# Attention scores of two layers from two extra projection columns, carried as bf16 pieces, in a four-layer graph network on one core

## What is computed

```
L0: h @ W;  e = leaky_relu(h@a[:D] + (h@a[D:])^T);  att = softmax(where(adj > 0, e, NEG), axis=1)
    elu(att @ (h @ W)) @ han_w + han_b
L1: e_r[i,j] = sum_d h[i,d] h[j,d] a_rel[r,d] + c_r;  the relation is chosen by adj; softmax; att @ h
L2: Wh = h @ W^T;  e = leaky_relu(Wh@a1 + (Wh@a2)^T);  softmax(where(adj == 0, NEG, e));  att @ Wh
L3: three steps of  m = h @ weight[i];  aggr = (adj != 0)^T @ m;  h = gru_cell(aggr, h)
```

## Time and profile before

| | us |
|---|---|
| median of 3 runs | 563.78 |
| lowest, highest | 562.48, 564.67 |
| the profiled execution's own time | 562.25 |
| its span (what the views show) | 560.5 |
| mean granted clock of TensorE | 0.97 |

### The profile page before, as it was taken

One profiled execution on the slowest core, in us unless ns is written; L12 is line 12 of the kernel. 1 busy time (PEld: TensorE's weight loads), 2 busy tenths in 40 slices (PEclk: granted clock), 3 DMA queues, 4 the chain that ended last, 5 costly groups with the idle time before them and its releaser, 6 DMA issues.

```text
span 560.5 us, 10803 instructions
## 1 busy us (share of the span) xinstructions
PE 515.1 (92%) x3262; PEld 439.1 (78%) x3280; DVE 429.4 (77%) x1436; ACT 408.8 (73%) x956; POOL 363.5 (65%) x314
## 2 busy tenths in 40 slices
PE   5857876899999999999999999999999999999964
PEld 5856665788888888888888888888888777868753
DVE  3636786788888898888888888888888887867633
ACT  1563565778887878788888888797888677767742
POOL 4241764777787878868687877777877666463330
PEclk9896998999999999999999999999999999999987
DMA  7980000000000000000000000000000000000001
GB/s 188 253 236 1 2 1 1 1 2 2 1 2 19 0 19 0 19 0 19 0 19 0 19 0 19 0 11 8 0 19 0 19 2 20 20 1 20 0 20 37
DMA packets 20893, 14.00 MB, mean 25 GB/s; under 512 B 2944, under 2 KB 18048, under 8 KB 20864
## 3 DMA queue, kind: packets, MB, share of 16 engines
q1 hardware_dynamic: 18944, 13.25, 8.5%
q10 hardware_dynamic: 1920, 0.40, 0.4%
HBM read 9.44 MB, written 4.19 MB: 24 GB/s over the span
## 4 chain that ended last, share of the span: by engine, by line
PE 67%; ACT 13%; DVE 8%; issue 5%; DMA 4%; POOL 2%; ACTq 1%; POOLq 0%; DVEq 0%; another core or an unknown queue 0%
PE ps_mix L1174 7%; PE ps_L L1053 7%; PE ps_L L1151 5%; ACT prob_L L485 4%; PE ps_r L1180 3%; PE ps_r L1182 3%; PE ps_z L1182 3%; PE ps_z L1180 3%; PE ps_r L1181 3%; PE ps_z L1181 3%; PE ps_mix L1053 3%; DVE xn_L L720 3%; PE ps_L L1131 3%; DMA above_row<-above 2%; PE ps_L L1159 2%
## 5 line engine op out<-in xcount | busy, mean ns | idle before, releaser
L720 DVE SCALAR_TENSOR_TENSOR xn_L<-x_sb,stats_L,rstd_L 128x128 f32<-128x128 f32 x256 | 86.6, 400 | 9.4 <-POOL rstd_L L359 6.9
L379 POOL TENSOR_TENSOR hT_lo<-hTf,hT_hi 128x512 fp32r<-128x512 f32 x32 | 44.8, 1399 | 66.4 <-ACT hT_hi L566 66.4
L374 POOL TENSOR_TENSOR diff<-hTf,gate_r 128x512 f32<-128x512 f32 x48 | 62.3, 1297 | 33.2 <-ACT gate_r L560 33.2
L485 ACT ACTIVATE prob_L<-prob_L,negm_L 128x128 f32<-128x128 f32 x192 | 74.3, 392 | 1.6 <-DVE negm_L L757 1.5
L359 POOL TENSOR_TENSOR rstd_L<-veps_L,minus_half 128x4 f32<-128x4 f32 x64 | 71.3, 1114 | 5.3
L403 POOL TENSOR_SCALAR mask_L<-adj_sb 128x512 bf16<-128x512 int32 (+1 forms) x32 | 65.9, 2058 | 2.7
L795 DVE TENSOR_TENSOR ag_lo<-ps_mix,ag_hi 128x512 fp32r<-128x512 f32 x48 | 33.2, 692 | 32.8 <-ACT ag_hi L533 32.8
L1174 PE MATMUL ps_mix<-adj_sb,hN 128*128 (+1 forms) x384 | 52.6, 281 | 1.0 <-ACT hN L572 0.8
L549 ACT ACTIVATE gate_r<-ps_r,bias_r 128x512 f32<-128x512 f32 x48 | 33.0, 687 | 27.1 <-PE ps_r L1182 25.6
L1174 PEld LDWEIGHTS ps_mix<-adj_sb,hN 128*128 128x128 f32 x384 | 49.6, 197 | 3.1 <-ACT hN L572 1.6
L757 DVE CUSTOM_DVE_ANT_0 prob_L<-ps_L,prob_L 128x128 f32<-128x128 f32 x192 | 44.0, 284 | 7.4 <-issue 7.3
(11 more groups left out here) (168 smaller groups left out, 1564.0 us busy)
## 6 DMA issues: line engine op xcount, KB each, us to landing
out_dram<-x_sb SPq DMA_DIRECT2D x16, 256.0 KB, 2.3
x_sb<-in_x_dram SPq DMA_DIRECT2D x1, 768.0 KB, 11.8
adj_sb<-in_adj_dram SPq DMA_DIRECT2D x1, 768.0 KB, 12.2
x_sb<-in_x_dram SPq DMA_DIRECT2D x2, 256.0 KB, 6.0
adj_sb<-in_adj_dram SPq DMA_DIRECT2D x2, 256.0 KB, 7.1
w_ih_sb<-in_L_gnn_w_ih_dram SPq DMA_DIRECT2D x1, 192.0 KB, 8.4
w_hh_sb<-in_L_gnn_w_hh_dram SPq DMA_DIRECT2D x1, 192.0 KB, 3.6
w_l_sb<-in_L_gnn_weight_dram SPq DMA_DIRECT2D x1, 192.0 KB, 3.2
```

What stands on the lines that cost most here:

```text
L374: nc.gpsimd.tensor_tensor(diff[k][:, :], hTf[k][:, :], gate_r[k][:, :], ALU.subtract).then_inc(diff_done[k], 1)
L379: nc.gpsimd.tensor_tensor(hT_lo[k + 1][:, :], hTf[k + 1][:, :], hT_hi[k + 1][:, :].bitcast(F32), ALU.subtract).then_inc(new_hT_lo[k], 1)
L485: last = nc.scalar.activation(part(prob[s], b), part(prob[s], b), ACT.Exp, bias=negm[s][:, b:b + 1], scale=-1.0, accum_out=psum_row[s][:, ...
L720: last = nc.vector.scalar_tensor_tensor(part(xn[s], b), graph(x_sb, g, b), stats[s][:, b, 1:2], rstd[s][:, b:b + 1].to_broadcast([P, D]), ...
```

## The change

The two score numbers per node now come from the projection. The weight of layers 0 and 2 gets two more columns (`w_aug`, 128x130: the weight, and the two score vectors times 0.2), so that one projection gives values and both numbers. ACT copies all of it to SBUF (`copy_projected`; before, only layer 2's values were copied). DVE splits the eight numbers per node and group (4 graphs x 2) into three bf16 pieces each (`split`: 4 operations that each wait for the one before). PE transposes the 24 columns with one bf16 matmul (`pieces_transposed`), ACT copies the 24x128 result (`copy_pieces`), and PE makes the outer sum with eight bf16 matmuls of 24 rows, against `chosen`, constant tiles of zeros and ones that pick a graph's pieces. The mask matmuls stay.

In layer 0, `normalise` becomes `centre`: one operation that subtracts the mean and does not wait for the inverse deviation. The deviation goes in later: into the score numbers (a fifth step ahead of the split) and into the inverse of the sum (a second operation in `inverse_sum`).

PSUM: a projection of 4 x 130 columns needs more than a bank, so it takes halves of two neighbouring ones. The banks of layer 0, `ps_in` and layer 2 lie side by side in `ps_row`; the projections of layers 0 and 2 both use `ps_in`'s, in turn with three candidate products per period.

The flag: PE sums the counts over the partitions with matmuls of one column (`count_above`), and no transfer is left. DVE compares the sum. The time terms of layer 1 are made right after `add_layer_0(0)`.

POOL: `edges_in_place` now subtracts layer 2's mask from ones and follows it; seven or so more steps at the start make the constant tiles. The waits that were on `wait_alone` are on the instructions themselves in `norm_stats` and `leaky`.

Order: all hardware loops are gone. Each engine's program is a written list of calls; groups 8 to 15 repeat one pattern, written once and unrolled when it is built, and the start and the end are lists of their own. The bank a step waits for is an argument of the call. Cut to its core:

```diff
-    MIX_USES = (("a2", 5), ("a1", 4), ("t2", 5), ("a3", 5), ("t3", 6), ("t1", 4))
...
+    DA = D + 2
+    HALF = 2 * DA
+    NP = 3
+    NR = GB * NP
...
-        ps = {"L0": bank("ps_L0"), "L1": bank("ps_L1"), "L2": bank("ps_L2")}
+        ps_row = ctx.enter_context(nc.psum_tensor("ps_row", [P, 3 * W], F32))
+        ps = {"L0": ps_row[:, 0:W], "L1": bank("ps_L1"), "L2": ps_row[:, 2 * W:3 * W]}
         ps_mix, ps_r, ps_z = bank("ps_mix"), bank("ps_r"), bank("ps_z")
-        ps_in, ps_hn = bank("ps_in"), bank("ps_hn")
+        ps_in, ps_hn = ps_row[:, W:2 * W], bank("ps_hn")
...
-            for a, b in FLAG_SUMS:
-                sp.wait_ge(s_above, b)
-                sp.dma_start(above_row[:, 0:(b - a) * P], above[:, a:b]).then_inc(s_above_row, 16)
...
-            with sp.Fori(0, NG) as g:
+            for g in range(NG):
                 store(g)
...
             def rsqrt(s, g):
                 pool.wait_ge(stats_done[s], g + 1)
+                if s == "L0":
+                    wait_from(pool, rinv_done["L0"], g)
                 nc.gpsimd.tensor_scalar(veps[s][:, :], stats[s][:, :, 2], 1.0 / D, EPS, ALU.mult,
-                                        ALU.add).then_inc(veps_done[s], 1)
-                pool.wait_ge(veps_done[s], g + 1)
+                                        ALU.add).then_inc(rstd_done[s], 1)
...
-                nc.gpsimd.tensor_scalar(group(adj_sb, g).bitcast(F32), group(adj_sb, g), 0, 0,
-                                        ALU.is_equal, ALU.is_equal).then_inc(edges_done, 1)
...
+                nc.gpsimd.tensor_tensor(group(adj_sb, g).bitcast(F32), all_ones[:, :],
+                                        mask["L2"][:, :], ALU.subtract).then_inc(edges_done, 1)
...
+            def copy_projected(s, g):
+                act.wait_ge(values_in_psum[s], g + 1)
+                if s == "L2":
+                    wait_from(act, mixed["L2"], g)
+                nc.scalar.activation(projected_sb[s].rearrange("p b c -> p (b c)")
+                                     .rearrange("p (h c) -> p h c", h=2), projected_half(s),
+                                     ACT.Copy).then_inc(values_copied[s], 1)
...
+            def copy_pieces(s, g):
+                act.wait_ge(pieces_in_psum[s], g + 1)
+                nc.scalar.activation(piecesT[s][:, :], ps[s][0:2 * NR, W - D:W], ACT.Copy)\
+                    .then_inc(piecesT_done[s], 1)
...
+            def centre(g):
+                dve.wait_ge(stats_done["L0"], g + 1)
+                wait_from(dve, xT_in_psum["L0"], g)
+                nc.vector.tensor_tensor(by_graph(xn["L0"][:, :]), by_graph(group(x_sb, g)),
+                                        stats["L0"][:, :, 1:2].to_broadcast([P, GB, D]),
+                                        ALU.subtract).then_inc(xn_done["L0"], 1)
...
+                if s == "L0":
+                    dve.wait_ge(rstd_done["L0"], 2 * (g + 1))
+                    nc.vector.reciprocal(inverse_0[:, :], psum_row["L0"][:, :])\
+                        .then_inc(inverse_0_done, 1)
+                    dve.wait_ge(inverse_0_done, g + 1)
+                    nc.vector.tensor_tensor(rinv["L0"][:, :], inverse_0[:, :], rstd["L0"][:, :],
+                                            ALU.mult).then_inc(rinv_done["L0"], 1)
...
+            def split(s, g, before, whole):
+                piece = [pieces[s][:, :, :, n] for n in range(NP)]
+                step = split_step[s]
+                nc.vector.tensor_scalar(piece[0], whole, 1.0, None, ALU.mult).then_inc(step, 1)
+                dve.wait_ge(step, before + 1)
+                nc.vector.tensor_tensor(parts_left[s][:, :, :], whole, piece[0], ALU.subtract)\
+                    .then_inc(step, 1)
+                dve.wait_ge(step, before + 2)
+                nc.vector.tensor_scalar(piece[1], parts_left[s][:, :, :], 1.0, None, ALU.mult)\
+                    .then_inc(step, 1)
+                dve.wait_ge(step, before + 3)
+                nc.vector.tensor_tensor(piece[2], parts_left[s][:, :, :], piece[1], ALU.subtract)\
+                    .then_inc(step, 1)
+            def score_pieces_0(g):
+                dve.wait_ge(values_copied["L0"], g + 1)
+                dve.wait_ge(rstd_done["L0"], 2 * (g + 1))
+                before = SPLIT_STEPS["L0"] * g + 1
+                nc.vector.tensor_tensor(score_parts[:, :, :], projected_sb["L0"][:, :, D:DA],
+                                        rstd["L0"][:, :].unsqueeze(2).to_broadcast([P, GB, 2]),
+                                        ALU.mult).then_inc(split_step["L0"], 1)
+                dve.wait_ge(split_step["L0"], before)
+                split("L0", g, before, score_parts[:, :, :].rearrange("p b t -> p t b"))
+            def score_pieces_2(g):
+                dve.wait_ge(values_copied["L2"], g + 1)
+                split("L2", g, SPLIT_STEPS["L2"] * g,
+                      projected_sb["L2"][:, :, D:DA].rearrange("p b t -> p t b"))
...
             def read_flag(n):
-                a, b = FLAG_SUMS[n]
-                dve.wait_ge(s_above_row, 16 * (n + 1))
-                after_prep(nc.vector.tensor_reduce(above_max[:, :], above_row[:, 0:(b - a) * P],
-                                                   AX.X, ALU.max))
-                after_prep(nc.vector.tensor_scalar(many[:, :], above_max[:, :], 0.5, None,
-                                                   ALU.is_gt))
+                dve.wait_ge(above_counted, n + 1)
+                after_prep(nc.vector.tensor_scalar(many[:, n:n + 1], ps_z[0:1, 3 * D:3 * D + 1], 0.5,
+                                                   None, ALU.is_gt))
...
+                for b in range(GB):
+                    last = nc.tensor.matmul(projected_half(s)[:, b // 2, (b % 2) * DA:(b % 2 + 1) * DA],
+                                            part(hT[s], b), w_aug[s][:, :], start=True, stop=True)
+                last.then_inc(values_in_psum[s], 1)
...
+            def pieces_transposed(s, g):
+                if s == "L0":
+                    keep_clock_up(8, g)
+                pe.wait_ge(split_step[s], SPLIT_STEPS[s] * (g + 1))
+                nc.tensor.matmul(ps[s][0:2 * NR, W - D:W],
+                                 pieces[s][:, :, :, :].rearrange("p t b q -> p (t b q)"),
+                                 unit_b[:, :], start=True, stop=True).then_inc(pieces_in_psum[s], 1)
+            def piece_scores(s, b, stop):
+                nc.tensor.matmul(part(ps[s], b), part(chosen[0], b), piecesT[s][:, :],
+                                 start=False, stop=False)
+                return nc.tensor.matmul(part(ps[s], b), piecesT[s][:, :], part(chosen[1], b),
+                                        start=False, stop=stop)
             def scores_0(g):
-                keep_clock_up(3, g)
-                pe.wait_ge(hT_done["L0"], g + 1)
+                pe.wait_ge(piecesT_done["L0"], g + 1)
+                pe.wait_ge(values_copied["L0"], g + 1)
                 pe.wait_ge(mask_done["L0"], g + 1)
-                if isinstance(g, int) and g == 0:
-                    pe.wait_ge(s_prep_dve, PREP_L0)
-                nc.tensor.matmul(ps["L0"][:, :], a_src_rep[:, :], hT["L0"][:, :], start=True,
-                                 stop=False)
+                if g == 0:
+                    pe.wait_ge(s_prep_pool, N_PREP_POOL)
                 for b in range(GB):
-                    nc.tensor.matmul(part(ps["L0"], b), part(hT["L0"], b), a_dst_rep[:, :],
-                                     start=False, stop=False)
-                for b in range(GB):
-                    last = nc.tensor.matmul(part(ps["L0"], b), part(mask["L0"], b), ident_b[:, :],
-                                            start=False, stop=(b == GB - 1))
+                    nc.tensor.matmul(part(ps["L0"], b), part(mask["L0"], b), ident_b[:, :],
+                                     start=True, stop=False)
+                    last = piece_scores("L0", b, True)
...
             def scores_2(g):
-                pe.wait_ge(values_done["L2"], g + 1)
+                pe.wait_ge(piecesT_done["L2"], g + 1)
+                pe.wait_ge(values_copied["L2"], g + 1)
                 pe.wait_ge(mask_done["L2"], g + 1)
-                nc.tensor.matmul(ps["L2"][:, :], w2a_dst_rep[:, :], hT["L2"][:, :], start=True,
+                nc.tensor.matmul(ps["L2"][:, :], ident_b[:, :], mask["L2"][:, :], start=True,
                                  stop=False)
                 for b in range(GB):
-                    nc.tensor.matmul(part(ps["L2"], b), part(hT["L2"], b), w2a_src_rep[:, :],
-                                     start=False, stop=False)
-                nc.tensor.matmul(ps["L2"][:, :], ident_b[:, :], mask["L2"][:, :], start=False,
-                                 stop=True).then_inc(scores_done["L2"], 1)
...
+                    last = piece_scores("L2", b, b == GB - 1)
+                last.then_inc(scores_done["L2"], 1)
...
+            def count_above(first, last):
+                pe.wait_ge(s_above, last)
```

(8 more changed lines are left out.)

1800 lines of the change are left out of this document (1374 added, 426 removed).

## The result

The changed kernel takes **570.23 us** (median of 4 runs, 568.90 to 571.65), the kernel before, beside it on the same chip, 563.67 (4 runs, 562.48 to 564.67). The ratio is 1.0118, 95% interval 1.0084 to 1.0151: slower by 1.2%, where 6.5% faster was forecast. The profiled execution took 569.54 us, its span is 567.8.

What follows compares the result with a forecast made beforehand. PE alone was taken to bound the middle; from 560.5 us of span, middle -20.9, head -9 and tail -7 gave 523.6, a median of 527 us. The range, 8 times in 10, was 510 to 542.

Steps and rivals of the forecast that it cites:

- rival 3: Split chains lie open on PE, up to 4.5 us per group against 2.43 saved: slower, 585 us; chance 0.03.
- DVE's sum: DVE per group: -1.35 normalise, +0.69 centre, +1.60 tiny operations; 26.45 us busy, 26.8 with waits, 98% of PE's 27.24.
- PE's term for the new blocks: PE score blocks per group: layer 0's 12 short matmuls 0.57 us, layer 2's 0.61, priced at the mask's 0.048 each.
- upper bound, 28.2: PE's period if the weight load is not hidden behind 18 short matmuls, 0.97 us more than 27.24.
- Head: Start of the run: flag stall about -3 us, higher clock about -3, better filled order -3; -9 (0 to -16).
- terms on the flag: Head: PE's 4.11 us stall at the flag goes but for the register load, about -3 us; clock afterwards, about -3.
- POOL's set-up steps: Head: new steps ahead of group 0's xb and deviation, covered by DVE's angle work; uncovered up to 2 us.
- Tail: End of the run: layer 2's scores of three groups -4 us, less idle -3; -7 (-2 to -12).
- Rival 1: DVE takes over as bound at 0.2 us per tiny operation: 28.9 us period, total 540; chance 0.2.
- Rival 4: Unrolled code stalls at each skipped relation block, +30 us over 16 skips, result 557; chance 0.03.
- rival 2: The order gives back more: PE period 27.24, head -14, tail -10, total 514; chance 0.13.

Runs made afterwards that it cites:

- e1: Changed kernel with POOL's two-input GRU steps (diff, hT_lo) on 128 of 512 columns from group 1 on, leaving out work; 549.99 us, 0.9737 of before.
- e5: Changed kernel with layer 0's mask matmuls ahead of its pieces, plus calls reordered on four engines in the loop and the lists behind it; 565.2 us.
- e10: e8 with calls reordered in the loops of four engines, the lists behind nearly as they were; 545.23 us, 0.9645 of before.
- e6: Changed kernel with group 0's inverse deviation made between POOL's constant tiles and ACT's sine behind elu of group 0; 571.13 us.
- e8: Changed kernel with pieces padded by zeros so every score matmul has 128 rows, timed again after a single run; 558.80 us, 0.9903 of before.
- e2: Changed kernel with POOL's diff and hT_lo steps reading one tensor instead of two, subtraction left out; 555.09 us, 0.9837 of before.
- e4: Changed kernel with only the first bf16 piece made, six of nine split operations left out; 554.89 us, 0.9828 of before.

## Why the prediction was wrong

The forecast was 527 (510 to 542), with 0.94 on faster; the result lies 43 us above it. Of the cases named, only rival 3 was slower than before, and its mechanism was not the one. By the marks the forecast was -14.9 us over seven periods of 27.6 and -22 outside them; it came out as +3.4 and +4.0.

1. **The step that failed: DVE's sum, "so 26.45 busy … 26.8. That is 98% of PE's 27.24".** It moved DVE's operations into a new order and kept the durations they had beside their old neighbours. The operations themselves were, if anything, priced too high: without the held time DVE needs 29.25 - 4.65 = 24.6 us per period, against 26.45 less the 1.1 that before had. The tiny ones were nearly right (0.17 us and 0.02 to 0.04 between them). What came in place of the sum is 4.6 us per period of standing still behind POOL, 3.5 more than before. e1 takes 1.47 us off the period (30.21 to 28.74) with no change to DVE; e5 and e10 remove most of the hold by order alone.
2. **PE's term for the new blocks was mis-sized**: 1.49 for 0.57 in layer 0 and 0.86 for 0.61 in layer 2. "I take the lower, since the masks run at 0.048 with just such loads" took a row of 128-row matmuls for a case that changes rows eight times. PE's need per period is e1's 28.74 us, in which it idles 0.14; the sum had 27.24, and its upper bound, 28.2, was too low. The blocks are 1.17 of the 1.5 missing; the rest was not measured piece by piece. So of the 2.6 us per period by which the forecast missed, 1.14 are PE's (27.6 to e1's 28.74) and 1.47 the hold: 18 us over seven periods.
3. **Head, forecast -9, measured +7.8 by the first mark.** Its terms on the flag came true in kind and were outweighed. PE's longest idle time near the flag is 1.97 us for 4.11, and from 40 to 60 us the granted clock is 0.90 for 0.74:

```profile
41.59 0.38 PE L1859 MATMUL ps_L<-mask_L,ident_b 128*128 128x512 bf16 x1 [1.97 <-ACT arhT L623]
```

Two terms of the head failed. POOL's set-up steps were taken as covered by DVE's angle work, 2 us at most if not: group 0's inverse deviation is ready at 14.2 us for 8.5, and its `add_layer_0` ends at 31.1 for 26.5 (e6 brings the first back to 8.7 us and gains nothing by the first mark). And the forecast had no loss of clock anywhere: in the stretches from 60, 80 and 100 us on, of 20 us each, it is 0.84, 0.66 and 0.83 where before had 1.00, 0.91 and 1.00. With 128 rows it is 1.00, 0.91 and 1.00 again, and e8 gets back 11.4 us; but e2 and e4 get back 8 of them with 24 rows, so how much the clock itself costs stays open. In e8 that mark is 3.8 us ahead of before's; the rest of the -9 is unexplained.
4. **Tail, forecast -7, measured -3.8 behind the eighth mark**, which includes some periods at the loop's rate. e1 has 6.7 us less there than the kernel after, but e1 also shortens POOL's own steps, so how much of that is the hold is not shown.
5. **Rival 1 was the right kind** (DVE takes over as the bound, chance 0.2), with the wrong price: it came from 0.2 us per tiny operation and gave 540. With the hold it is 30.21 us of period. What spoke against it, "in the middle before it never held PE up", was read from an order that the change replaced.
6. **Rival 3** (split chains open) did not decide. PE's wait for the pieces, in the view of waits of the kernel after (us in total, times, longest), is 0.87 us per group over the whole run, and 0.70 per period from 180 to 390 us, against the 2.43 it needed:

```profile
PE ps_row L1834 <- DVE pieces_L L1248: 14.0, 15, 3.1
```

7. **Rival 4** (stalls at skipped blocks) did not show: e10 unrolls as much and runs its period at 27.99.
8. One slip in the sums changes nothing: rival 2's terms give 515 by the forecast's own steps, not 514.

What stays open: e10's 545 is 18 us above 527. 2.7 us of them lie in the seven periods (28.0 for 27.6 each), 16 outside: ahead of the first mark and behind the eighth e10 gained 2.9 us each on before. That a better list for the end would bring more is only argued from e5, where a worse one cost 13 us.

## What to carry to other kernels

A mean duration in a profile belongs to the order it was taken in. Before moving DVE or POOL work, look at the shortest, median and longest of each operation and at what lies beside the longest, and put DVE's PSUM-reading operations and statistics beside POOL's two-input steps (e5 and e10 took the hold from 4.6 to 0.9 and 1.7 us that way). And price a matmul of an unusual shape by a run with its neighbours, not by the nearest row: the change of shape cost more than the matmul.

## What the runs showed of the hardware that was not expected

- A 0.68 us DVE operation took 1.77 beside a POOL step of 1.66; four of 0.35 took 3.22 beside two such steps. With that step reading one tensor, the longest was 1.10 (e2).
- A change between 24-row and 128-row bf16 matmuls costs PE about 0.1 us (0.15 from start to start, against 0.057 to 0.07); matmuls of 24 rows are no shorter than those of 128 (0.06 to 0.07 from start to start in the kernel after, 0.057 in e8).
- With 24-row matmuls in the head the granted clock was 0.79 to 0.86 from 20 to 120 us in nine kernels, with 128 rows 0.91 to 0.95 in four; the kernel before, which has none of them, has 0.93. Each is one execution.
- A DVE operation on 8 elements took 0.17 us, about as one on a single element, and one with two per-partition numbers (TENSOR_SCALAR) 343 ns on 128x128, as the two-tensor form.
